# The fp4 layer of the last batch placed inside the differential attention's block, its gated rows transposed tile by tile, and the output stored in pieces

## What is computed

```python
# differential attention, per head: two softmaxes, 256-wide values
A1 = einsum('bhqd,bhkd->bhqk', Q1, K1) * scaling
A2 = einsum('bhqd,bhkd->bhqk', Q2, K2) * scaling
attn = softmax(A1) - lam * softmax(A2)
O = einsum('bhqk,bhkd->bhqd', attn, V)
O = O / sqrt(mean(O * O) + EPS) * rms_scale * (1.0 - LAMBDA_INIT)
x = x + einsum('bne,de->bnd', O, Wo)
# fp4 layer: I = 352, H = 128, blocks of 16 along the last axis
def fp4_quant_dequant(x):
    scale = maximum(max(abs(xb)) / 6.0, 1e-12)
    return nearest_of_grid(xb / scale) * scale
gate, up = q(z) @ q(w_gate).T, q(z) @ q(w_up).T
x = x + q(silu(gate) * up) @ q(w_down).T
```

## Time and profile before

| | before |
|---|---|
| median of three runs (us) | 3026.27 |
| the profiled execution (us) | 3022.49 |
| its span, first to last instruction (us) | 3020.7 |
| TensorE busy, share of the span | 93% |
| VectorE busy | 79% |
| ScalarE busy | 63% |
| GpSimd busy | 21% |
| mean granted TensorE clock | 0.97 |
| DMA out, one transfer of 2048 KB, issue to landing (us) | 8.7 |

### The profile page before, as it was taken

How to read it: one execution, slowest core, us unless ns; L and a number is a source line. 1 busy time by engine, 2 the same in 40 slices (tenths; PEclk the granted TensorE clock), 3 DMA queues, 4 the chain that set the end, 5 groups by cost and what they waited for, 6 DMA issues and landing times. The chain is left out here.

```text
span 3020.7 us, 50344 instructions
## 1 busy us (share of the span) xinstructions
PE 2806.0 (93%) x14514; PEld 1773.0 (59%) x14514; DVE 2379.6 (79%) x3991; ACT 1897.2 (63%) x3759; POOL 636.6 (21%) x1246
## 2 busy tenths in 40 slices
PE   4799999999789998899999999999999999999984
PEld 2122222222478887677777777777777777777762
DVE  6999989998455554777777888888788888888865
ACT  5388878888732322566666666666666666666651
POOL 4100000000100000033333333333233333333330
PEclk9699999999999999999999999999999999999996
DMA  2220000000010000000000000000000000000000
GB/s 75 73 78 23 22 14 23 23 23 2 1 57 1 1 1 1 1 1 0 0 0 1 1 1 0 0 1 1 2 1 0 0 1 1 1 0 0 0 1 28
DMA packets 30934, 34.72 MB, mean 11 GB/s; under 512 B 7576, under 2 KB 18816, under 8 KB 30592
## 3 DMA queue, kind: packets, MB, share of 16 engines
q1 hardware_dynamic: 30720, 32.18, 3.6%
HBM read 23.37 MB, written 8.39 MB: 11 GB/s over the span
## 5 line engine op out<-in xcount | busy, mean ns | idle before, releaser
L1682 DVE TENSOR_REDUCE neg_maxima<-ps 128x1 f32<-128x1024 f32 x512 | 624.7, 1220 | 157.8 <-PE ps L1537 144.2
L1642 ACT ACTIVATE diff_probs<-ps,neg_maxima 128x1024 f32<-128x1024 f32 x512 | 573.9, 1121 | 172.0 <-DVE neg_maxima L1682 171.6
L666 ACT ACTIVATE probs<-ps 128x512 f32<-128x512 f32 x1024 | 535.2, 605 | 176.0 <-PE ps L729 175.8
L582 DVE TENSOR_REDUCE maxima_of_halves<-ps 128x2 f32<-128x1024 f32 x512 | 601.6, 1219 | 17.7 <-PE ps L686 12.9
L1534 PE MATMUL ps<-z_T_high,y_high 128*128 (+1 forms) x1024 | 481.9, 471 | 11.5 <-issue 5.4
L1482 PE MATMUL ps<-arena,z_tiles 128*128 128x512 f32 x1024 | 460.6, 592 | 0.0
L1535 PE MATMUL ps<-z_T_low,y_high 128*128 (+1 forms) x1024 | 405.7, 396 | 0.0
L1589 ACT COPY arena<-ps 128x512 f32<-128x512 f32 x512 | 299.2, 584 | 107.6 <-PE ps L1469 86.1
L1896 POOL TENSOR_SCALAR mean_squares<-square_sums 128x1 f32<-128x1 f32 x256 | 119.7, 467 | 1074.8 <-ACT squares L1604 1074.6
L729 PE MATMUL ps<-q_stacks,k_stacks 51*128 51x512 bf16 x1024 | 314.9, 386 | 22.9 <-ACT probs L666 14.7
L1694 DVE SCALAR_TENSOR_TENSOR D<-diff_probs,ratio 128x1024 f32<-128x1024 f32 x256 | 328.9, 1285 | 9.2 <-DVE ratio L1690 0.2
(11 more groups left out here) (288 smaller groups left out, 4009.9 us busy)
## 6 DMA issues: line engine op xcount, KB each, us to landing
q_stacks<-q_parts_dram SPq DMA_DIRECT2D x192, 32.0 KB
q_parts_dram<-qk_parts SPq DMA_DIRECT2D x12, 256.0 KB, 2.4
k_parts_dram<-qk_parts SPq DMA_DIRECT2D x12, 256.0 KB, 3.4
k_stacks<-k_parts_dram SPq DMA_DIRECT2D x32, 96.0 KB
residual<-in_L_attn_x_dram SPq DMA_DIRECT2D x4, 512.0 KB, 6.1
k_stacks<-k_parts_dram SPq DMA_DIRECT2D x32, 64.0 KB
out_dram<-residual SPq DMA_DIRECT2D x1, 2048.0 KB, 8.7
q_stacks<-neg_max_parts SPq DMA_DIRECT2D x96, 4.0 KB, 1.7
```

Of the source, the lines that this page charges most:

```text
L582: nc.vector.tensor_reduce(mx_half[:, own, half, :, p * PB + t, :], ps[:, bank:bank + 2, :], X, ALU.max).then_inc(nat_max, 1)
L666: nc.scalar.activation(probs[:, k % PT, h, :], ps[:, (r + k + i) % S_RING, :], ACT.Exp, scale=SCALE).then_inc(s_free, 1)
L1642: nc.scalar.activation(probs[:, t % 2, m, :], ps[:, 2 * m:2 * m + 2, :].rearrange("p k n -> p (k n)"), ACT.Exp, bias=neg[:, t, m:m + 1], a ...
L1682: nc.vector.tensor_reduce(neg[:, t, m:m + 1], ps[:, 2 * m:2 * m + 2, :].rearrange("p k n -> p (k n)"), X, ALU.max, negate=True).then_inc(m ...
```

## The change

Five things are done. (1) The function `fp4_phase` and its block are gone; its parts become methods of a class `LastTiles`, and the engines call them inside `differential_phase`'s `finish()`, from the middle of the attention's remainder on. Group 0 (the last batch's tiles 0 to 3) is begun on VectorE once `add` has done these four tiles, ahead of `low_u` and of the adds of tiles 4 to 7. (2) `finish()` is no longer a loop over k but an order for each engine: the transposes of the last `D` tiles and the gate turn come ahead of the projections, and the turns `HT` and `Y` of fp4 tile 23 come later. GpSimd makes the weights of two tiles at a time. (3) The product by the block scale is four instructions of 128x352, each releasing one tile for `transpose_h`. `round_h(1)` waits for group 0's transposes only at these products, and its steps are spread between the multiplies and adds. (4) `down` writes one tile to one of two banks, and `add` takes one tile. (5) `store_phase` is gone: SyncE stores each of the first three batches once its tiles are done, then tiles 0 to 3, 4 to 5 and 6 to 7 of the last batch. Buffers of the heads alone (`MH`, `ML`, `yH`, `yL`, `probs`) are set free for those of `LastTiles`, so that some tiles lie at other SBUF addresses; the heads' own instructions are as before.

```diff
...
+                def finish():
                     it = B * H
-                    if k == 0:
-                        pe.wait_ge(s_free, 2 * it * PB + S0)
-                    project(it * PB + k - PB, k, H - 1, it * 2 - 2 + k // G, k % G)
-                    if k < 2:
-                        for j in range(2):
-                            transpose_D(it * PB - 2 + k, PB - 2 + k, j)
-                    if k in LAST_GROUP:
-                        sum_values(it * 2 - 1, 1, LAST_GROUP[k], it * 4)
-                    fp4_turns(it, k, False, True)
+                    n, tile = it * PB, it - FIRST - 1
+                    project_last = lambda k: project(n + k - PB, k, H - 1, it * 2 - 2 + k // G, k % G)
+                    for j in range(2):
+                        transpose_D(n - 2, PB - 2, j)
+                    pe.wait_ge(s_free, 2 * n + S0)
+                    fp4_turn(tile, TURN_GATE)
+                    project_last(0)
+                    project_last(1)
+                    fp4_turn(tile, TURN_UP)
+                    for j in range(2):
+                        transpose_D(n - 1, PB - 1, j)
+                    project_last(2)
+                    project_last(3)
+                    for part in range(2):
+                        sum_values(it * 2 - 1, 1, part, it * 4)
+                    for k in range(G, PB):
+                        project_last(k)
+                    fp4_turn(tile, TURN_HT)
+                    tail.transpose_z(pe, 0)
+                    pe.wait_ge(o_free, n + O0)
+                    pe.wait_ge(dt_out, 2 * n + DT0)
+                    for m in range(tail.G):
+                        tail.project(pe, m)
+                        if m == 0:
+                            fp4_turn(tile, TURN_Y)
+                    tail.transpose_z(pe, 1)
+                    for m in range(tail.G, tail.N):
+                        tail.project(pe, m)
+                    pe.wait_ge(f_free, (tile + 1) * TURNS + 1)
+                    pe.wait_ge(u_free, it * 2 + U0)
+                    for g in range(tail.GROUPS):
+                        for m in range(g * tail.G, (g + 1) * tail.G):
+                            tail.transpose_h(pe, m)
+                            if m % tail.G:
+                                tail.down(pe, m - 1)
+                        tail.down(pe, m)
...
+                def finish():
                     it = B * H
-                    fp4_turns(it, k, False, True)
-                    square(it * PB + k - PB, k, k % G)
-                    if k < 2:
-                        for j in range(2):
-                            copy_DT(it * PB - 2 + k, PB - 2 + k, it * 2 - 1, j)
-                    if LAST_GROUP.get(k) == 1:
-                        copy_u(it * 2 - 1, 1)
+                    n = it * PB
+                    square_last = lambda k: square(n + k - PB, k, k % G)
+                    fp4_turns(it, 0, False, True)
+                    for j in range(2):
+                        copy_DT(n - 2, PB - 2, it * 2 - 1, j)
+                    fp4_turns(it, 1, False, True)
+                    square_last(0)
+                    square_last(1)
+                    for j in range(2):
+                        copy_DT(n - 1, PB - 1, it * 2 - 1, j)
+                    square_last(2)
+                    square_last(3)
+                    copy_u(it * 2 - 1, 1)
+                    for k in range(G, PB):
+                        square_last(k)
+                    fp4_turns(it, 5, False, True)
+                    tail.copy_z(act, 0)
+                    for m in range(tail.G):
+                        tail.silu(act, m)
+                    tail.copy_z(act, 1)
+                    for m in range(tail.G, tail.N):
+                        tail.silu(act, m)
+                    for m in range(tail.N):
+                        tail.copy_h(act, m)
...
+                def finish():
+                    it = B * H
+                    n = (it - 1) * PB
+                    add_last = lambda k: add(n + k, k, B - 1, k % G)
+                    combine(n + PB - 1, PB - 1, H - 1)
+                    end_tile(it, 2)
+                    for k in range(G):
+                        add_last(k)
+                    dve.wait_ge(o_free, n + G + O0)
+                    tail.moments(dve, 0)
+                    end_tile(it, 3)
+                    tail.z_rows(dve, 0)
+                    low_u(it * 2 - 1, 1)
+                    tail.z_scaled(dve, 0)
+                    add_last(G)
+                    add_last(G + 1)
+                    tail.z_rounded(dve, 0)
+                    add_last(G + 2)
+                    add_last(G + 3)
+                    dve.wait_ge(o_free, n + PB + O0)
+                    tail.moments(dve, 1)
+                    tail.pad(dve)
+                    end_tile(it, 6)
+                    tail.z_rows(dve, 1)
+                    tail.multiply(dve, 0)
+                    tail.multiply(dve, 1)
+                    tail.z_scaled(dve, 1)
+                    tail.z_rounded(dve, 1)
+                    tail.multiply(dve, 2)
+                    tail.multiply(dve, 3)
+                    tail.h_shrunk(dve, 0)
+                    tail.h_scaled(dve, 0)
+                    tail.multiply(dve, 4)
+                    tail.multiply(dve, 5)
+                    tail.h_rounded(dve, 0)
+                    tail.multiply(dve, 6)
+                    tail.multiply(dve, 7)
+                    tail.h_shrunk(dve, 1)
+                    tail.add(dve, 0)
+                    tail.add(dve, 1)
+                    tail.h_scaled(dve, 1)
+                    tail.add(dve, 2)
+                    tail.add(dve, 3)
+                    tail.h_rounded(dve, 1)
+                    for m in range(tail.G, tail.N):
+                        tail.add(dve, m)
...
+                def weights_of_two(n, t):
+                    c = slice(t, t + 2)
+                    step = stepper(pool, weigh, 4 * n)
+                    wait_first(pool, sq_done, n + 2)
+                    step(pool.tensor_scalar(mean[:, c], ssq[:, c], 1.0 / (2 * DH), None, ALU.mult))
+                    pool.nop(nofuse=True)
+                    step(pool.tensor_scalar(mean[:, c], mean[:, c], EPS, None, ALU.add))
+                    step(pool.tensor_tensor(root[:, c], mean[:, c], core.minus_half[:, 0:2], ALU.pow))
+                    pool.tensor_tensor(root[:, c], root[:, c], inv[:, c, 0], ALU.mult).then_inc(weigh, 5)
+                def finish():
+                    n = (B * H - 1) * PB
+                    weights_of_two(n, 0)
+                    weights_of_two(n + 2, 2)
+                    norm_rstd(f_norm, pool, 0)
+                    weights_of_two(n + 4, 4)
+                    weights_of_two(n + 6, 6)
+                    norm_rstd(f_norm, pool, 1)
...
+                for b in range(B - 1):
+                    sp.wait_ge(f_free, (b + 1) * PB * TURNS + 1)
+                    store(b * PB, PB)
+                last = (B - 1) * PB
+                sp.wait_ge(tail.y_done, G)
+                store(last, G)
+                for n in range(G, PB, 2):
+                    sp.wait_ge(tail.y_done, n + 2)
+                    store(last + n, 2)
+                sp.wait_ge(stored, 16 * (B - 1 + 1 + (PB - G) // 2))
...
+    def h_rounded(self, dve, g):
+        fp4_rounded(dve, self.rounder, stepper(dve, self.hs, g * self.H_STEPS + FP4_SCALED))
+        for t in range(self.G):
+            if g:
+                dve.wait_ge(self.h_psum, (g - 1) * self.G + t + 1)
+            fp4_times_scale(dve, self.rounder, self.h4[:, t:t + 1, 0:self.fp4.I], t, 1).then_inc(self.hs, 1)
+    def add(self, dve, n):
+        dve.wait_ge(self.y_psum, n + 1)
+        dve.tensor_tensor(self.x(n), self.core.ps[:, self.Y[n % 2], 0:self.core.C], self.x(n), ALU.add).then_inc(self.y_done, 1)
...
+    def transpose_h(self, pe, n):
+        g, t = divmod(n, self.G)
+        if n == 0:
+            pe.wait_ge(self.padded, 1)
+        pe.wait_ge(self.hs, g * self.H_STEPS + FP4_STEPS + t)
+        if n >= 2:
+            pe.wait_ge(self.hT_free, n - 1)
+        for j in range(self.fp4.J):
+            ins = pe.transpose(self.core.ps[:, self.HT + n % 2, j * P:(j + 1) * P], self.h4[:, t, j * P:(j + 1) * P], self.core.ident[:])
+        ins.then_inc(self.h_psum, 1)
+    def down(self, pe, n):
+        pe.wait_ge(self.hT_free, n + 1)
+        if n >= 2:
+            pe.wait_ge(self.y_done, n - 1)
+        for j in range(self.fp4.J):
+            ins = pe.matmul(self.core.ps[:, self.Y[n % 2], 0:self.core.C], self.h4T[:, n % 2, j * P:(j + 1) * P], self.fp4.wd[:, j, :],
+                            start=j == 0, stop=j == self.fp4.J - 1)
+        ins.then_inc(self.y_psum, 1)
...
-        differential_phase(core, diff_weights, fp4, rows)
-        fp4_phase(core, fp4, core.tiles - core.per_batch)
-        store_phase(core, out)
+        differential_phase(core, diff_weights, fp4, rows, out)
```

(29 more changed lines are left out.)

263 lines of the change are left out of this document (97 added, 166 removed).

## The result

The median of the changed kernel is 2992.97 us (2987.81 to 2996.34, 4 runs), against 3024.85 us (3021.55 to 3028.3, 4 runs) of the kernel before in the same series: the ratio is 0.9893, with a 95% interval from 0.9874 to 0.9912, or 31.9 us. The forecast was 2998.2 us and a gain of 28.1.

What follows compares the result with a forecast made beforehand. TensorE, busy 93% of 3020.7 us, bounds the heads, which the change leaves alone; 101.1 us follow them. Gains 4.1 + 9.45 + 0.4 + 7.7 + 6.45 = 28.1 us off 3026.27 give 2998.2 us, range 2993 to 3006.

Steps and rivals of the forecast that it cites:

- the new wait for `Y`: VectorE, before fp4 tile 23's addition, waits 3.5 us for the turn that TensorE does behind group 0's `z` transposes and projection.
- (a): Attention's remainder with group 0's first half in it: last adds end 4.1 us sooner, and group 0's `z`, 9.45 us, is done.
- The three terms up to the last add: Attention's remainder: adds ending sooner 4.1 us, group 0's `z` done by then 9.45, engines' meeting between the blocks gone 0.4.
- (b): Stretch from `moments(1)` to the last addition: 55.5 us becomes 47.8, a gain of 7.7 us.
- (c): Store at the end: only a 128 KB piece, about 2.0 us, comes after the last addition; gain 6.45 us.
- the lower end itself, -5: Most the unknown costs could take off: final chain and products before `Y` at TensorE's higher clock, halving 7.2 + 3.7 us.
- the unknown costs: Dearer handovers +4, TensorE's clock at most -5 or +5.6, a transfer 0.5; together -5 to +8 us.
- GpSimd held up by VectorE: Rival: GpSimd groups VectorE waits for cost 0.7 us more each, 4.2 to twice that; 3003 to 3006 us; chance 0.09.
- The overlap eaten by handovers: Rival: waits in TensorE's and ScalarE's fixed orders use up the 9.45 us; gain 18.7, time 3007.6 us; chance 0.12.
- Longer heads: Rival: new buffer addresses or SyncE's stores lengthen the 256 slots; 0.15 us each gives 3036.6 us; chance 0.03.

Runs made afterwards that it cites:

- the run with ten unread products: Changed kernel plus ten TensorE products nobody reads, between the first group's down products and the second's transposes; tail 69.6 us, 2.5 us shorter.

## Why the prediction was right and where it was wrong

Its steps, counted from the start of the last `D` (2918.29 before, 2922.38 after), since the two profiles arrive there 4.1 us apart:

| place | predicted | measured |
|---|---|---|
| gated row of fp4 tile 23 and its scales | 4.7 | 4.6 |
| adds 0 and 1 | 5.6 | 5.6 |
| adds 2 and 3 | 9.2 | 9.0 |
| `low_u` | 15.3 | 15.0 |
| the last add | 23.5 | 23.7 |
| the new wait for `Y`, its length | 3.5 | 3.5 |
| multiply 1 | 31.3 | 31.2 |
| `z_rounded(1)` | 36.7 | 36.5 |
| the last product by the scale of group 0 | 51.1 | 50.7 |
| the last down product of group 1 | 71.0 | 69.6 |
| end of the span | 74.3 | 72.1 |

The **overlap**, (a) in the prediction, is as forecast, to 0.4 us at each place up to 36.5: VectorE's order keeps it busy while GpSimd, TensorE and ScalarE make what it needs next. The three terms up to the last add, 4.1 + 9.45 + 0.4 = 13.95 us, measured 37.5 - 23.75 = 13.7, from the last `D`'s start to the moments of group 1. Group 0 done late shows that its placement is worth 7.0 us of the tail; the rest is the new order around it.

The step that failed is the **term of (b)**, the stretch from `moments(1)` to the last addition. It was put at 7.7 us and measured 9.4: 3011.24 - 2955.76 = 55.5 before and 2992.24 - 2946.13 = 46.1 after. The mechanism was right, the size was not, and the 1.7 us lie in small pieces. I took 0.555 us for each 128x352 product by the scale, the distance of steps that wait for one another; these four don't, and took 1.83 together, (1.83 - 0.52) / 3 = 0.44 from one to the next: 0.4 us. The first four additions of 128 columns stood in my working with 1.4 us, some waiting for TensorE included; from 2976.83 to 2977.24 and from 2978.89 to 2979.29 they took 0.8, and none of them waited: 0.6 us. The last chain took 6.9 and not 7.2: 0.3 us. It was not at 0.50 throughout, before or after (0.74 from 3007 to 3011 in the old kernel, 0.76 from 2988 to 2992 in the new one); the clock only rose sooner in the new one, so that the last three transposes took 0.53 us (2989.88 above) where the old ones took 0.85:

```profile
3008.16 0.85 PE L2124 MATMUL ps<-identity,fp_h_rounded 128*128 128x128 f32 x3
```

The rest is the net of smaller ones: multiply 1 came 0.3 us sooner behind the last add, and multiply 5 waited 0.68 us where I had some 0.4.

The **term of (c)**, 6.45 us, measured 7.2: from the last addition's end to the end of the span it is 9.5 before and 2994.5 - 2992.24 = 2.3 after. A piece of 128 KB lands in 1.8 us, not 2.0; its bounds, 1.5 and 2.4, had held it. The two transfers ahead of it, for which I had taken off 0.25, cost nothing that shows. The last 0.3 I had overlooked: the old store was issued 0.28 us behind the last addition, in a block of its own, and without the block it follows at once (0.03 us in the variant with one store). The slope that I read from the earlier trace rows is 3.6 us for 1024 KB and not 3.5, which changes nothing here.

Together the tail came out 2.2 us shorter than predicted. The other 3.0 us of the 5.2 are not in the change. 1.4 are the start of the reckoning: the median of three runs of the kernel before, 3026.27, became 3024.85 with a fourth; further series gave 3025.23, 3025.72 and 3023.94. The remaining 1.6 is within the changed kernel's own scatter, 2995.13 us in a second series.

**The range** did not make up for these two terms. With (b) and (c) at their measured sizes the forecast would have been 2.4 us lower, and 2992.97 inside a range of the same width. And the lower end itself, -5, is short of what I had listed: half of 7.2 + 3.7 is 5.45, with 0.5 for the transfer 5.95, which gives 2992.2. (The size of that item was wrong too, the other way: at the higher clock the last chain lost 2.0 us in the run with ten unread products, not 3.6.) Besides, the unknown costs were all in the tail, but what lies ahead of it differs from profile to profile by up to 6.7 us (1235.4 to 1242.1) with the clock that TensorE is granted there, and a median over a few runs keeps a microsecond or two of that. That had to be added. The numbers were at hand: the three runs shown lay 4.9 us apart.

The **rivals**: GpSimd held up by VectorE: a pair's weight took 1.8 us (2925.38 to 2927.17) beside an idle VectorE and 2.4 (2941.44 to 2943.86) beside the fp4 steps:

```profile
2926.97 0.20 POOL L2011 TENSOR_TENSOR out_weight<-out_weight,inverse_sums 128x2 f32<-128x2 f32 x1
...
2941.44 0.24 POOL L2007 TENSOR_SCALAR mean_squares<-square_sums 128x2 f32<-128x2 f32 x1
...
2942.14 0.97 POOL L2010 TENSOR_TENSOR out_weight<-mean_squares,minus_half 128x2 f32<-128x2 f32 x1
2943.26 0.60 POOL L2011 TENSOR_TENSOR out_weight<-out_weight,inverse_sums 128x2 f32<-128x2 f32 x1
```

So 0.6 us dearer, near the 0.7 of the earlier trace rows, and the instructions at 2942.14 and 2943.26 are the ones that grow (0.72 and 0.20 us for the first pair). With group 0 done late, no fp4 steps run beside that last pair, and it took 1.7 us. But the adds that need it start at 2945.29, so nobody waited. The Trainium skill's rule of the shared port pair (SBUF — State Buffer, "SBUF: two separate sides") points at the right instructions; the cover, which the rule does not speak of, decided. The overlap eaten by handovers: no, except at `Y`, whose wait was in the sum. Longer heads: 1680.3 against 1681.1 us, so no lengthening by addresses or stores; all profiles of the changed kernel and its variants lie between 1679.9 and 1680.3, but for one at 1678.1, and the two of the old kernel's order at 1681.1 and 1681.4. That the heads are 1 us shorter I can't explain; the early stores are not it, since they stand in the 1681.4. The two banks for `down`, too, had no run of their own.

## What to carry to other kernels

When a serial end is folded into the block ahead of it, follow the one engine that issues most of its work, row by row, with what the other engines deliver in between: that gave every place here within half a microsecond up to the last group of tiles, and the end 2.2 us too late, by the sizes of (b) and (c). Compare kernels of which only an end differs by that end's length in the profile, since what lies ahead of it can differ by more than the edit is worth. Even then look at the places in between: of the 2.6 and 2.5 us by which two variants here shortened the end, 1.3 and 0.5 went with TensorE's clock at places where the edit is not shown to act. And put a turn that has its data ahead of one that still waits for them: one line's place on TensorE cost 1.3 to 2.0 us here.

## What the runs showed of the hardware

Stores from SBUF took 1.8, 2.3, 3.2 and 8.7 us from issue to landing for 128, 256, 512 and 2048 KB, a straight line of about 3.6 us for 1024 KB above 1.4. Three stores of 512 KB under matmul-bound work lengthened it by 0.3 us at most (1680.3 with one store, 1679.9 to 1680.3 with six in nine of ten profiles and 1678.1 in the tenth; 1681.1 and 1681.4 on the old order). VectorE's instructions of 128x352 follow at 0.56 us when each waits for the one before, and at 0.44 when it doesn't. And the clock that TensorE gets in the same code differs between runs, 0.91 and 0.85 in one stretch of 100 us, and with it the whole time by some microseconds. In a last chain of transposes, copies and products it decides 2.0 us: 6.9 us at 0.50 and then 0.76, behind 6.2 us in which TensorE stood idle, and 4.9 us at 1.00, behind ten products that filled that gap.
